# First self-attention of a two-layer decoder: scores and maximum on row halves of the array, a head in four equal steps

## The reference

```python
xq = einsum('bsh,oh->bso', x, wq); xk = ...; xv = ...      # 16 heads of 64
xq = xq.reshape(bsz, N_HEADS, seqlen, HEAD_DIM)            # also xk, xv
scores = einsum('bhid,bhjd->bhij', xq, xk) * HEAD_DIM ** -0.5
out = einsum('bhij,bhjd->bhid', softmax(scores), xv)
return einsum('bso,ho->bsh', out.reshape(bsz, seqlen, 1024), wo)
# then x = layernorm(x + attention(x))
```

## Time and profile before

| what | us |
|---|---|
| median of the runs | 2968.56 |
| span of the profiled execution, the only time that its page gives | 2978.0 |
| TensorE busy | 2631.8 (88%) |
| VectorE busy | 1704.5 (57%) |
| GpSimd busy | 1621.4 (54%) |
| ScalarE busy | 1190.8 (40%) |

### The profile page before, as it was taken

The page is one execution under the profiler, slowest core; times in us unless marked ns, Lnnn a source line. Parts: engine busy times, 40 slices in busy tenths (PEclk is TensorE's granted clock), DMA queues, the critical chain, the costliest instruction groups (busy, mean ns, idle before and its releaser), DMA issues. The chain is left out here.

```text
span 2978.0 us, 43667 instructions
## 1 busy us (share of the span) xinstructions
PE 2631.8 (88%) x12081; PEld 1634.0 (55%) x12081; DVE 1704.5 (57%) x3436; ACT 1190.8 (40%) x1678; POOL 1621.4 (54%) x1343
## 2 busy tenths in 40 slices
PE   7999999999999999999999968982795588798695
PEld 5666666666666666666666534441574244454254
DVE  5666666656666666665666635662234555468743
ACT  3444444444444444444444324541222333454234
POOL 3666776767766677676776753424334313333343
PEclk8999999999999999999999979996897599899798
DMA  6565455555446445455544320003993100000232
GB/s 176 113 136 113 105 120 113 123 115 114 109 113 138 108 109 121 109 122 114 118 112 108 76 68 23 2 2 126 343 347 128 41 0 1 30 2 9 61 116 88
DMA packets 407010, 303.20 MB, mean 102 GB/s; under 512 B 293558, under 2 KB 338910, under 8 KB 401790
## 3 DMA queue, kind: packets, MB, share of 16 engines
q1 hardware_dynamic: 390734, 231.17, 33.1%
q0 software_dynamic: 12224, 64.71, 6.1%
q10 hardware_dynamic: 3952, 6.08, 0.6%
HBM read 187.04 MB, written 94.39 MB: 95 GB/s over the span
## 5 line engine op out<-in xcount | busy, mean ns | idle before, releaser
L655 POOL TENSOR_TENSOR a_total<-a_total,a_pr 128x1024 f32<-128x1024 f32 x384 | 914.8, 2382 | 46.1 <-ACT a_pr L639 23.4
L639 ACT ACTIVATE a_pr<-a_psS 128x1024 f32<-128x1024 f32 x512 | 525.3, 1027 | 657.3 <-PE a_psS L627 657.3
L584 DVE TENSOR_REDUCE a_nmax<-a_psX 128x1 f32<-128x512 f32 x1024 | 694.2, 687 | 139.9 <-PE a_psX L579 137.8
L667 PE MATMUL a_psO<-a_pr,a_vd 128*64 128x512 f32 x2048 | 481.8, 602 | 0.0
L579 PE MATMUL a_psX<-a_kA,a_qA 128*128 128x512 f32 x1024 | 415.8, 408 | 17.3 <-issue 6.2
L655 POOL TENSOR_TENSOR a_total<-a_pr 128x1024 f32<-128x1024 f32 x64 | 153.3, 2396 | 487.9 <-ACT a_pr L639 487.9
L627 PE MATMUL a_psS<-a_qA,a_kA 128*128 128x512 f32 x1024 | 339.1, 412 | 2.5 <-DVE a_nT L600 1.4
L627 PE MATMUL a_psS<-a_qB,a_kB 128*128 128x512 f32 x1024 | 322.1, 396 | 0.0
L667 PEld LDWEIGHTS a_psO<-a_pr,a_vd 128*64 128x64 f32 x2048 | 129.9, 136 | 239.6 <-issue 188.1
L579 PEld LDWEIGHTS a_psX<-a_kA,a_qA 128*128 128x128 f32 x1024 | 193.9, 189 | 102.2 <-DVE a_nmax L584 23.5
L627 PEld LDWEIGHTS a_psS<-a_qA,a_kA 128*128 128x128 f32 x1024 | 181.2, 189 | 121.5 <-issue 90.1
(11 more groups left out here) (400 smaller groups left out, 4517.5 us busy)
## 6 DMA issues: line engine op xcount, KB each, us to landing
a_qA<-a_qhi SPq DMA_DIRECT2D x124, 256.0 KB
a_vd<-a_vg SPq DMA_DIRECT2D x128, 128.0 KB
a_kA<-a_khi SPq DMA_DIRECT2D x62, 256.0 KB
a_kA<-a_klo SPq DMA_DIRECT2D x62, 256.0 KB
a_kB<-a_khi SPq DMA_DIRECT2D x62, 256.0 KB, 5.6
a_qB<-a_qlo SPq DMA_DIRECT2D x62, 256.0 KB, 5.9
a_qhi<-a_ph SPq DMA_DIRECT2D x120, 128.0 KB, 3.2
a_qlo<-a_pl SPq DMA_DIRECT2D x120, 128.0 KB, 2.7
```

Source lines behind the costliest of these rows:

```text
L584: w.eng.tensor_reduce(nmax[:, half, u:u + 1], psX[:, half, :], AX.X, ALU.max, negate=True)\
L639: w.eng.activation(pr[:, n, :], psS[:, half, :, :].rearrange("p a b -> p (a b)"), ACT.Exp, scale=SCALE)\
L655: w.eng.tensor_tensor(total[:, buf, :], first, pr[:, n, :], ALU.add).then_inc(sems["ad"], 1)
L667: last = w.eng.matmul(psO[q * HD:(q + 1) * HD, :], vd[:, b, kc, :], pr[:, n, q * 512:(q + 1) * 512], start=kc == 0, stop=kc == KC - 1)
```

## The change

- `largest` runs eight times a head, not 16. It issues two matmuls of 64 rows, high Q by high K only: rows 0-63 (qA, kA) for keys 0-511 into `psX[0]` and rows 64-127 (qA, kB) for keys 512-1023 into `psX[1]`. VectorE reduces 1024 columns at once. The next step waits for that reduction (`room(w, "0", "1")`).
- Scores are written as products of 64 rows, in pairs on the two row halves that go to different banks. Two chunks k0 and k1 form a step; each bank's second products wait by the semaphore `half` until the first of the pair's bank are done.
- A head is four equal steps: scores of two chunks, two maximum steps, values of the two chunks before (the last two chunks of a head fall into the next head), and tasks.
- One transpose and one copy in `max_rows`, not two and a minimum.
- `came` remembers for each bank which result has to have left it; task banks alternate ("1M", "M10M").
- `build` is split: three key DMAs at step 1, nine more at step 3, all of half size. Eight, not five, Q/K tasks are ahead of the group.

```diff
-        def largest(w, i, b, back=None):
+        def largest(w, u, b, first=False):
             if w.on("tensor"):
-                w.wait("mxr", w.at("mxr", 1))
-                w.eng.matmul(psX[:, half, :], qA[:, b, u * P:(u + 1) * P], kA[:, b, half * 512:(half + 1) * 512],
-                             start=True, stop=True).then_inc(sems["mx"], 1)
...
+                room(w, "0", "1")
+                w.eng.matmul(psX[:, 0, :], qA[0:HD, b, u * P:(u + 1) * P], kA[0:HD, b, 0:512], start=True, stop=True)
+                w.eng.matmul(psX[:, 1, :], qA[HD:P, b, u * P:(u + 1) * P], kB[HD:P, b, 512:1024], start=True, stop=True)\
+                    .then_inc(sems["mx"], 1)
...
+                w.eng.tensor_reduce(nmax[:, u:u + 1], psX[:, :, :].rearrange("p a k -> p (a k)"), AX.X, ALU.max, negate=True)\
...
+        def score(w, what, kc, q, b):
+            rows = slice(0, HD) if what in (HIHI, MAXIMUM) else slice(HD, P)
+            kt, qt = (kA, qA) if what in (HIHI, HILO) else (kB, qB)
+            first = what == (HIHI, HILO)[q]
+            last = what == (LOHI, MAXIMUM)[q]
+            return w.eng.matmul(psS[:, kc % 2, q, :], kt[rows, b, kc * P:(kc + 1) * P], qt[rows, b, q * 512:(q + 1) * 512],
+                                start=first, stop=last)
+        def scores(w, p, b, nb, first=False):
+            k0, k1 = 2 * p, 2 * p + 1
+            if w.on("tensor"):
+                room(w, "S0", "S1")
+                w.wait("e", w.at("e", 1))
+                score(w, HIHI, k0, 0, b)
+                score(w, HILO, k0, 1, b)
...
+                score(w, MAXIMUM, k0, 0, b)
+                score(w, LOHI, k0, 1, b).then_inc(sems["half"], 1)
+            if nb is not None:
+                largest(w, k0, nb, first)
...
+                w.wait("half", w.at("half", 1))
+                score(w, HIHI, k0, 1, b)
+                score(w, HILO, k0, 0, b)
+                score(w, MAXIMUM, k0, 1, b)
+                score(w, LOHI, k0, 0, b).then_inc(sems["s"], 1)
+                w.wait("half", w.at("half"))
...
+            if nb is not None:
+                largest(w, k1, nb, first)
...
+        PLACES = [(3, 0), (3, 0), (3, 2), (3, 2), (3, 3), (3, 3), (3, 3), (3, 3), (0, 0), (0, 0), (0, 3), (0, 3), (0, 3), (0, 3),
+                  (1, 0), (1, 0)]
+        TASKS[0, 2], TASKS[1, 2], TASKS[2, 2] = [("V", 0, 0)], [("V", 0, 1)], [("V", 1, 0), ("V", 1, 1)]
+        TASKS[1, 3], TASKS[2, 3] = [("O", 1)], [("T",), ("O", 0)]
+        BANKS = {("QK", 2): "1M", ("QK", 4): "M10M", ("V", 1): "M", ("V", 2): "1M", ("O", 1): "M", ("T", 2): "1M"}
...
+                for p in range(KC // 2):
+                    scores(w, p, b, nb if more else None, first and j == 0)
...
+                    if p == 0:
+                        if old:
+                            values(w, KC - 2, nb)
+                            values(w, KC - 1, nb)
+                            take_out(w)
...
+                    else:
+                        values(w, 2 * p - 2, b)
+                        values(w, 2 * p - 1, b)
+                    if p == 1 and old:
+                        misc(w, ("S",), G, (j + 1) % 2)
...
+                    if p == 3 and more:
+                        max_rows(w)
+                        masked(w, nb, 0)
...
```

More of the change, by code:

```diff
@@ L50, in loop @@
         self.count = dict(start)
+        came = {k: (n, v - per[n]) for k, (n, v) in self.came.items()}
+        self.came = dict(came)
         with eng.Fori(0, trips) as reg:
@@ L55, in loop @@
         self.count = {k: start.get(k, 0) + trips * n for k, n in per.items()}
+        self.came = {k: (n, v + trips * per[n]) for k, (n, v) in came.items()}
 class Writer(Tally):
@@ L393, in load_x, with room, misc @@
             w.inc("x", 32)
-        def misc(w, what, G, buf, more=True, bank=None, back=(0, 0), out=True):
+        def room(w, *places):
+            least = {}
+            for name, value in (w.came[k] for k in places if k in w.came):
+                least[name] = max(least.get(name, 0), value)
+            for name, value in least.items():
+                w.wait(name, w.at(name, w.count[name] - value))
+        def misc(w, what, G, buf, k="M", more=True, out=True):
             kind = what[0]
-            ps = psM if bank is None else bank
+            ps = bank[k]
             if w.on("tensor"):
-                w.wait("md", w.at("md", back[0]))
-                w.wait("ma", w.at("ma", back[1]))
+                room(w, k)
                 if kind == "T":
@@ L412, in misc @@
                     w.wait("xl", w.at("xl"))
-                    if c == 0:
+                    if c == 0 and not out:
                         w.wait("wl", 1 if kind == "Q" else 2)
@@ L420, in misc @@
                     _, tt, c2 = what
-                    w.wait("wl", 3)
+                    if not out:
+                        w.wait("wl", 3)
                     w.wait("xl", w.at("xl"))
@@ L529, in norm_out, with halves, build_keys @@
             w.inc("yo", 16)
+        def halves(t, rows, b, h):
+            return t[rows:rows + HD, b, h * 512:(h + 1) * 512].bitcast(F32)
+        def build_keys(w, G, j, b):
+            if w.on("sync"):
+                row = w.fixed(G * (GH * P) + j * P)
+                if j == 0:
+                    w.waits(("sg", AHEAD * 2 * 16), ("sh", (PIECES - AHEAD) * 2 * 16), *((f"so{n}", w.at(f"so{n}")) for n in range(PIECES)))
+                w.waits(("s", w.at("s")))
+                for t, rows, src in ((kB, HD, khi), (kA, 0, khi), (kA, HD, klo)):
+                    w.eng.dma_start(halves(t, rows, b, 0), src[bass.ds(row, HD), :]).then_inc(sems[f"a{b}"], 16)
+            w.inc(f"a{b}", 3 * 16)
         def build(w, G, j, b):
@@ L583, in largest, with max_rows @@
                 w.wait("mx", w.at("mx"))
-                w.eng.tensor_reduce(nmax[:, half, u:u + 1], psX[:, half, :], AX.X, ALU.max, negate=True)\
+                w.eng.tensor_reduce(nmax[:, u:u + 1], psX[:, :, :].rearrange("p a k -> p (a k)"), AX.X, ALU.max, negate=True)\
                     .then_inc(sems["mxr"], 1)
             w.inc("mxr")
-        def max_rows(w, b):
+            w.came["0"] = w.came["1"] = ("mxr", w.count["mxr"])
+        def max_rows(w):
             if w.on("tensor"):
[L592 to L595, removed]
+                room(w, "0")
+                w.eng.transpose(psX[0:KC, 0, 0:P], nmax[:, :], ident[:, :]).then_inc(sems["mt"], 1)
             w.inc("mt")
@@ L609, in masked @@
                 w.eng.tensor_tensor(qB[0:KC, b, cols].rearrange("p (u q) -> p u q", q=P),
-                                    nT[:, 1, :].unsqueeze(1).to_broadcast([KC, KC // 2, P]),
+                                    nT[:, :].unsqueeze(1).to_broadcast([KC, KC // 2, P]),
                                     rowmask[:, half * (KC // 2):(half + 1) * (KC // 2), :], ALU.mult).then_inc(sems["mb"], 1)
             w.inc("mb")
-        def scores(w, kc, b, a):
-            half = kc % 2
-            if w.on("tensor"):
[L618 to L633, removed]
@@ L702, in group, with tasks @@
             last = left == 0
+            def tasks(j, p):
+                ahead = 2 if j == 3 else 1
+                out = []
+                for task in TASKS.get((j, p), []):
+                    if task[0] == "O":
+                        if not (first and j == 1):
+                            out.append((task, G - (j == 1), task[1]))
+                    elif task[0] == "T":
+                        if left >= 2:
+                            out.append((task, G + 2, 0))
+                    elif ahead <= left:
+                        out.append((task, G + ahead, 0))
+                return out
             for j in range(GH):
@@ L707, in group @@
                 old = not (first and j == 0)
[L708 to L720, removed]
@@ L735, in group @@
[L735 to L744, removed]
-                            norm_out(w, G - (j == 1), 1 if j == 1 else 0)
-                        if kc == KC - 1 and not (last and j >= 2):
-                            build(w, G + (j + 2) // GH, (j + 2) % GH, b)
-                        step(2 * kc + 1)
-                        if outs and kc == 1:
-                            moments(w, 1 if j == 1 else 0)
-                        piece(f"k{kc}")
-                        if old and kc == 4:
-                            turn_back(w)
-                        if old and kc == 5:
-                            divide(w, (j - 1) % GH)
-                    if p == 1:
-                        piece("1")
-                    if p in (1, 2):
+                normal = j == 3 or (j == 2 and not first)
@@ L791, in group @@
-                piece("3e", bank=psX[:, 1, :], under=tuple(a + b - c for a, b, c in zip(after_3, past_3, past_3b)))
-                if j == 1 and not last:
-                    load_x(w, G + 2)
+                    if p == 1 and old:
+                        misc(w, ("S",), G, (j + 1) % 2)
+                    todo = tasks(j, p)
```

(20 more changed lines are left out.)

161 lines of the change are left out of this document (81 added, 80 removed).

## The result

The changed kernel takes 3011.64 us (median of 4 runs, 3009.18 to 3013.61) against 2968.77 for the one before: a ratio of 1.0143, interval 1.0129 to 1.0158. It is 43 us slower; the forecast was 17 us faster. The profiled execution spans 3011.9 us. The cross attention behind the stage starts 42.1 us later than before in the profiles (1806.39 against 1764.33), so nearly the whole difference lies in the first self-attention.

What follows compares the result with a forecast made beforehand. The prediction took TensorE's stream of matmuls as the bound. Its terms summed to -1.4 us per group, times 16 is -22, and +5 for edges: -17 us, a median of 2952 us (-0.57%), range 2870 to 3040.

Steps and rivals of the forecast that it cites:

- the hidden edits: Edits outside TensorE's path (order of exponentials, GpSimd's additions, smaller DMAs, build_v's wait), claimed to be covered and priced at nothing.
- The slower rival: At "half" and the reduction, TensorE stands until the event, then shows full load and start-up: 3003 to 3054 us, chance 0.26.
- (1): Maximum matmuls: 16 full slots per head become 8 half-height pairs, each fitting one slot: -7.4 us per group.
- (3): TensorE's old waits for VectorE in the loop vanish with the new order: -1.9 us per group.
- (6): Second wide maximum step of each step waits for the 1.23 us reduction: a 0.22 us hole, 16 times, +3.5 per group.
- (7): VectorE reaches the wide reduction late after four Q/K tasks: 0.38 us in two heads, +0.7 per group.
- (4): Values run in four blocks per head instead of three, each block's overhead 0.35 us: +1.4 us per group.
- (5): Switch from full-height tasks to row-half scores in 11 of 16 steps, 0.17 us each: +1.9 per group.
- (8): TensorE's waits on its own "half" between a bank's first and second score products: 0.03 us, +0.5 per group.
- (9): Edges: slower maximum steps before the first group, more DMAs to wait for, later last values: +5 us in all.
- the 0.3 for pairs that overrun a slot: Half-height pairs taken at 0.233 us, slightly over a slot's 0.23: +0.3 us per group.

Runs made afterwards that it cites:

- e1: The changed kernel with one semaphore for each V buffer, so values wait for their own V alone: 2961.22 us, ratio 0.9949.
- e5: e1 with scores as full-height products of 128 rows again, only the maximum in row halves: 3011.48 us in one run.
- e8: e1 with both mask products reading maxima from PSUM, without the copy, and ahead of the tasks' subtractions: 2930.82 us, ratio 0.9871.
- e6: e1 with the first maximum step one slot earlier and GpSimd adding only 32 of 1024 columns of chunks 6 and 7: 2878.97 us in one run.
- e7: e1 with the first maximum step one slot earlier and mask products reading PSUM, without the copy, ahead of the subtractions: 2885.43 us, ratio 0.9724.
- e2: The changed kernel with the load of x issued behind the V load in the third head, strict wait kept: 2971.98 us, ratio 0.9994.
- e4: e1 with the maximum reduced in two reductions of 512 columns, the second half's maxima left unused: 2977.10 us, ratio 1.0003.

## Why the prediction was wrong

The step that failed is the last sentence of the hidden edits: "build_v's stricter wait stands one step earlier than its need." It was priced at nothing. It looked at what V is needed for, and not at what the wait counts. The values' wait takes in the V load that the program has issued last, and that had moved ahead of it. Its price is 4.0 us in most groups. e1 takes away this wait alone and is 58 us faster than the change, 15 us faster than the kernel before: -17 + 58 = +41, of the 43 measured. The fall of the clock, 1.7 of the 4.0 us, stood nowhere in the forecast. The forecast also said that TensorE idle for a DMA in the loop would make it wrong; that is what came.

The slower rival was right in sign and wrong in mechanism: "half" costs nothing and the reduction what was priced.

The other steps, as measured:
- (1) Pairs fit a slot: 0.23 us, forecast 0.233. (3) With e1, TensorE's waits for VectorE that remain are those of (6) and (7).
- (4), (5) A switch costs 0.2 us: a step after tasks starts its second pair at 503.43, 0.34 after the first, where a slot is 0.23, and 0.1 lies ahead of the first. Forecast 0.17; e5 gives 0.2 too.
- (6) 1.223 us for the wide reduction (forecast 1.23) and 0.22 for the hole (0.22).
- (7) Mis-sized. In e1, 14 of a group's 16 steps have 1.72 us between their maximum steps, and the two behind four Q/K tasks 2.46 and 2.20: 1.2 us a group beyond (6), where 0.7 was priced. The cause is the mask product, taken as 0.69 and in the change 0.89 to 1.62 us at these places; with it short (e8) the spacing is 1.71 to 1.76 everywhere and a group 1.1 us shorter. The trace of the kernel before had the sign: one product of 1.17 to 1.26 us in most groups, beside a GpSimd addition. The forecast called GpSimd far from the bound and did not ask what it holds up.
- (8) Forecast 0.03, measured none.
- (9) The first scores start at 64.76 against 56.33; less 2.1 us for three tasks that moved there, 6.3, where 5 were given for all edges.
- Sum with e1: a group of 104.87 against "about 104.7", and -15 us against -17. That is closer than the terms are: (7) is 0.5 too small and (5) 0.3 (11 x 0.2 = 2.2), (8) is 0.5 too large and the 0.3 for pairs that overrun a slot was not needed. That these cancel is luck.

## What to carry to other kernels

When a load moves ahead of a wait in program order, look at what the wait's count now takes in: a counter shared by two buffers makes the consumer wait for the producer's next item. Price an engine's work at its new place also by what the other engines do at that time: look in the trace for the same instruction beside them. And where two things delay the same event, remove both before judging either.

## What the runs showed of the hardware

- VectorE's product of two SBUF operands (8 x 512) takes 0.67 us alone. When it starts beside a GpSimd addition in SBUF, it ends 0.54 to 0.55 us after that addition's end (126 products in the change, 19 in the kernel before; mean length of all in the change 1.61). With GpSimd idle it is 0.675 (e6), and with one operand in PSUM 0.674 beside GpSimd (e7). The subtractions and reductions that read PSUM never slowed (at most 0.43 and 1.23 us).
- Two products of 64 rows on the two row halves, in different banks and each with its own weight load, run in 0.23 us, the time of one of 128 rows, for whole steps. A switch between full height and row halves costs 0.2 us (e5).
- After the hole of 2.3 us TensorE worked on at 2.4 GHz for about a microsecond, then some 3.4 us at 1.2 GHz (granted clock from 559 us on, by microseconds: 0.76, 0.50, 0.50, 0.54, 1.00). After two of 13 such holes the clock did not fall, and after holes of 0.2 to 0.6 us (e1, e2) it never did in the loop.
- Two VectorE reductions back to back start 0.61 us apart though each is 0.69 long (e4).
